# Output projection by chunks onto a residual in PSUM, and other places in the queues

## The reference

```python
x = norm(x + random_feature_attention(x))          # ln1
x = norm(x + cross_attention(x, ctx))              # ln2: 16 heads, 120 keys
x = norm(x + three_cycles_of_coupling(x))          # ln3: gelu nets, out += coupling * twist(out)
# ln4: the state-space part
xr = x @ W_in.T;  x_ssm, res = split(xr)           # 512 channels each
xc = silu(conv4(x_ssm));  delta = softplus(xc)
h[n] = exp(-exp(A_log[n]) * delta) * h[n] + xc*xc  # a scan over the sequence, 16 states
y = xc * sum_n(h[n]) * silu(res) + D * xc
x = norm(x + y @ W_out.T)
x = norm(x + (gelu(x @ ctx.T) * (x @ ctx.T)) @ ctx)  # ln5
x = norm(x + gate * expert[argmax(router(x))](x))  # ln6: 8 experts, all computed
```

## Time and profile before

| what | value |
|---|---|
| median of 3 runs | 3413.72 us (3413.61 to 3415.29) |
| profiled execution, its own time | 3415.3 us |
| span, first to last instruction | 3413.5 us, 41544 instructions |
| busy share of the span: PE, DVE, ACT, POOL | 76%, 74%, 50%, 44% |
| mean granted clock of PE | 0.827 of 2.4 GHz |
| a loop turn | 201.4 us |
| DMA | 45.72 MB, 13 GB/s over the span |

### The profile page before, as it was taken

The page is one execution under the profiler, slowest core; times in us unless marked ns, Lnnn a source line. Parts: engine busy times, 40 slices in busy tenths (PEclk is TensorE's granted clock), DMA queues, the critical chain, the costliest instruction groups (busy, mean ns, idle before and its releaser), DMA issues.

```text
span 3413.5 us, 41544 instructions
## 1 busy us (share of the span) xinstructions
PE 2603.7 (76%) x10956; PEld 1509.9 (44%) x10956; DVE 2515.0 (74%) x4320; ACT 1722.0 (50%) x3078; POOL 1492.6 (44%) x1159
## 2 busy tenths in 40 slices
PE   4985787868778786877878688687877878787556
PEld 2544444444445443444444344444444445444323
DVE  2258678696877869687786968778696886859683
ACT  1456454546546464564646455454655545456430
POOL 1036354463525446253543625355362544526370
PEclk8767798888888888888888889888887988869677
DMA  3000000000000000000000000000000000000000
GB/s 118 10 7 9 13 10 13 15 13 6 9 19 9 13 12 3 19 9 19 9 13 12 3 19 9 13 15 13 12 3 19 9 13 6 7 6 0 12 5 8
DMA packets 16849, 45.72 MB, mean 13 GB/s; under 512 B 2248, under 2 KB 7056, under 8 KB 16400
## 3 DMA queue, kind: packets, MB, share of 16 engines
q1 hardware_dynamic: 16656, 43.96, 3.8%
HBM read 35.57 MB, written 8.39 MB: 13 GB/s over the span
## 4 chain that ended last, share of the span: by engine, by line
PE 47%; DVE 24%; issue 13%; ACT 12%; DVEq 1%; POOL 1%; ACTq 0%; DMA 0%; SPq 0%; POOLq 0%
PE bank L522 45%; DVE h_ring L1065 10%; ACT a_ring L1447 6%; DVE x L1163 2%; DVE smax L969 2%; PE bank L404 1%; ACT spare L1347 1%; DVE qT L1019 1%; DVE couple L1016 1%; DVE x12T L1021 1%; POOL ysum L1635 1%; DVE soft L1044 1%; DVE ln_stats L378 1%; DVE x L396 1%; ACT L1453 1%
## 5 line engine op out<-in xcount | busy, mean ns | idle before, releaser
L1635 POOL TENSOR_TENSOR ysum<-ysum,h_ring 128x512 f32<-128x512 f32 x896 | 1150.3, 1284 | 723.0 <-DVE h_ring L1065 660.3
L1065 DVE TENSOR_TENSOR_SCAN h_ring<-a_ring,bank 128x512 f32<-128x512 f32 x1024 | 1170.0, 1198 | 53.6 <-POOL ysum L1635 43.3
L522 PE MATMUL bank<-w_expert_w,x45T 128*128 128x512 f32 x1024 | 578.3, 712 | 228.1 <-DVE x L1163 226.6
L1447 ACT ACTIVATE a_ring<-soft,decay 128x510 f32<-128x510 f32 x1024 | 651.3, 707 | 25.7 <-DVE h_ring L1065 24.0
L522 PEld LDWEIGHTS bank<-w_expert_w,x45T 128*128 128x128 f32 x1024 | 223.8, 227 | 534.2 <-DVE x L1163 288.4
L1622 POOL TENSOR_TENSOR soft<-xc,soft 128x512 f32<-128x512 f32 x64 | 82.1, 1294 | 748.7 <-ACT soft L1418 748.7
L522 PE MATMUL bank<-x3T,w_winT 128*128 128x512 f32 x512 | 276.3, 673 | 22.5 <-ACT x3T L410 13.1
L522 PE MATMUL bank<-spare,w_cn_w 128*128 128x256 f32 x768 | 235.2, 444 | 74.5 <-ACT spare L1377 64.5
L1163 DVE SCALAR_TENSOR_TENSOR x<-bank,weight,x 128x256 f32<-128x256 f32 x512 | 213.3, 472 | 65.7 <-PE bank L522 65.7
L522 PE MATMUL bank<-qT,kmask 32*120 32x256 f32 x1024 | 215.3, 513 | 57.4 <-ACT spare L1347 56.8
L969 DVE TENSOR_REDUCE smax<-bank 128x4 f32<-128x480 f32 x256 | 156.2, 651 | 118.7 <-PE bank L522 118.7
(11 more groups left out here) (145 smaller groups left out, 4069.2 us busy)
## 6 DMA issues: line engine op xcount, KB each, us to landing
x0T<-in_xT SPq DMA_DIRECT2D x16, 512.0 KB, 3.2
x<-in_x SPq DMA_DIRECT2D x16, 512.0 KB, 3.4
out<-x SPq DMA_DIRECT2D x16, 512.0 KB, 2.8
ctxT<-in_ctxT SPq DMA_DIRECT2D x16, 240.0 KB, 2.5
ctxTb<-in_ctxT SPq DMA_DIRECT2D x16, 240.0 KB, 2.6
ctxb<-in_ctx SPq DMA_DIRECT2D x16, 240.0 KB, 3.0
w_expert_w<-in_expert_w SPq DMA_DIRECT2D x1, 2048.0 KB
w_winT<-in_winT SPq DMA_DIRECT2D x1, 1024.0 KB
```

Source lines behind the costliest of these rows:

```text
L522: return pe.matmul(o, l, r, start=start, stop=stop)
L1065: scanned.then(v.tensor_tensor_scan(h_ring[:, k % HRING, :], a_ring[:, k % RING, :, :].rearrange("p b s -> p (b s)"), xc2, 0.0, ALU.mult, ...
L1447: a.activation(a_ring[:, k % RING, :, 1:S], delta[:, c, :].rearrange("p (b s) -> p b s", b=NB)[:, :, 1:S], ACT.Exp, scale=decay[:, k:k + 1 ...
L1635: p.tensor_tensor(out=total, in0=first, in1=h_ring[:, k % HRING, :], op=ALU.add)\
```

## The change

The output projection goes by channel chunks instead of by tiles. At the end of a turn, after the last coupling cycle and ahead of rotate_back(f, 0), PE puts the residual of m into the banks MB by a product of the identity with the tensor of ln3 (two of 128 x 512), and adds the first three chunks to it. At the head of the next turn it adds the fourth chunk alone. keep and DVE's adds fall away; DVE takes the statistics of ln4 from PSUM and normalises out of PSUM. Beside the waits on the loads two are new: DVE's norm_apply of ln3 waits until PE has read the residual, and PE's transposes of ln4 wait for all four tiles.

Other places in the queues: the last tile of the input projection comes ahead of the last two score tiles; gated_out comes inside the loop of slots (k = 1), and expert_bias behind that loop and the first feature product; ACT's spread of ln4 (norm_rstd) comes ahead of the second input tile's copy; softplus of the last two chunks comes later in ACT's queue, and decays go on between the slots; DVE has other steps of PLAN done between its other work, the last two expert sums and ln6's statistics behind all scans; POOL adds the last two deltas in between its sums; squares are made at the decays 0, 18, 43 and 59. The weights are loaded under three semaphores: five tensors first, then the group's inputs, then those of cross attention and coupling with the head rows, then the rest.

```diff
+DELTA_AFTER = {13: 2, 18: 3}
 OUT_AFTER = 4
-SQUARE_AT = (0, 20, 34, 48)
+SQUARE_AT = (0, 18, 43, 59)
...
+FIRST = ["rfwT", "projT", "rows", "columns", "ident"]
+FRONT = ["wk", "wv", "wq", "wo", "cn_w1", "cn_w2", "cn_w3", "cn_w4", "gc_w1", "gc_w2", "gc_w3"]
+REST = [name for name in WEIGHTS if name not in FIRST + FRONT]
...
+            load_weights(FIRST, loaded_first)
             load_xT(0)
             load_keys(0)
             load_x(0)
+            load_weights(FRONT, loaded_front)
+            sp.dma_start(head_rows[:, :, :], ins["head_rows"]).then_inc(loaded_front.sem, 16)
+            load_weights(REST, loaded_rest)
             load_back(0)
...
-            def mamba_out(g, k0, k1):
...
-                    last = mm(MB[t // 2][:, t % 2 * D:t % 2 * D + D], yT[:, c, t // 2, t % 2 * P:t % 2 * P + P],
-                              woutT[:, c, :], c == 0, c == IC - 1)
-                    if t % 2 and c == IC - 1:
-                        last.then_inc(n4.sub_ready.sem, 1)
+            def mamba_out(g, c0, c1):
+
+                if c0 == 0:
+                    pe.wait_ge(expert_added.sem, expert_added.at(g, 0))
+                    pe.wait_ge(n3.x_ready.sem, n3.x_ready.at(g, NT))
+                    for h in range(2):
+                        mm(MB[h][:, :], ident[:, :], n3.x[:, 2 * h:2 * h + 2, :].rearrange("p t d -> p (t d)"),
+                           True, False).then_inc(resid_ready.sem, 1)
+                for c in range(c0, c1):
+                    pe.wait_ge(scanned.sem, scanned.at(g, AFTER["out", c, 0]))
+                    for t in range(NT):
+                        last = mm(MB[t // 2][:, t % 2 * D:t % 2 * D + D], yT[:, c, t // 2, t % 2 * P:t % 2 * P + P],
+                                  woutT[:, c, :], False, c == IC - 1 and t % 2 == 1)
+                        if t % 2 and c == IC - 1:
+                            last.then_inc(n4.sub_ready.sem, 1)
...
-                    mamba_out(b, 0, 16)
+                    mamba_out(b, IC - 1, IC)
...
+                    pe.wait_ge(n4.x_ready.sem, n4.x_ready.at(b, NT))
                     norm_turn(pe, n4, b, MB)
...
-                    turn_maxima(f)
+                    scores(f, 5, 6)
                 if m is not None:
                     mamba_in(m, b, 7, 8)
-                if b is not None:
-                    gated_out(b)
+                if f is not None:
+                    scores(f, 6, 8)
+                    turn_maxima(f)
                 for k in range(SLOTS + 2):
                     if f is not None:
                         attend(f, k, k + 1)
                     if b is not None:
-                        if k == 7:
+                        if k == 1:
+                            gated_out(b)
+                        elif k == 7:
                             norm_turn(pe, n5, b, MB)
                         elif k == 9:
                             router(b)
                         elif k == 13:
                             turn_weights(b)
-                        elif k == 15:
-                            expert_bias(b)
...
                 if b is not None:
-                    experts(b, 0, 1)
+                    expert_bias(b)
...
                 if b is not None:
-                    experts(b, 1, 2)
+                    experts(b, 0, 2)
...
+                if m is not None:
+                    mamba_out(m, 0, IC - 1)
+                if f is not None:
                     rotate_back(f, 0)
...
             def ln4_sum(g):
-                v.wait_ge(kept_ready.sem, kept_ready.at(g, 1))
-                norm_add(v, n4, g, [(tiles(MB[h]), n4.x[:, 2 * h:2 * h + 2, :]) for h in range(2)])
-                norm_stats(v, n4, g)
+
+                n4.chain.start(v, g)
+                for t in range(NT):
+                    v.wait_ge(n4.sub_ready.sem, n4.sub_ready.at(g, t // 2 + 1))
+                    n4.chain.then(v.bn_stats(n4.stats[:, t, :], MB[t // 2][:, t % 2 * D:t % 2 * D + D]))
...
+            def ln4_apply(g):
+                v.wait_ge(n4.rstd_ready.sem, n4.rstd_ready.at(g, 1))
+                for t in range(NT):
+                    v.tensor_scalar(n4.x[:, t, :], MB[t // 2][:, t % 2 * D:t % 2 * D + D], n4.mv[:, t, 0:1],
+                                    n4.rstd[:, t:t + 1], ALU.subtract, ALU.mult).then_inc(n4.x_ready.sem, 1)
...
+                states(m, 1)
+                if f is not None:
+                    copy_maxima(f)
+                states(m, 3)
                 if b is not None:
                     gated(b)
-                if f is not None:
-                    copy_maxima(f)
-                states(m, 4)
+                states(m, 6)
                 if b is not None:
                     ln5_sum(b)
-                states(m, 6)
+                states(m, 8)
                 if b is not None:
                     norm_apply(v, n5, b)
-                states(m, 9)
+                states(m, 12)
                 if f is not None:
                     normalize_context(f, 0)
-                states(m, 10)
+                states(m, 14)
                 if b is not None:
                     route(b)
-                states(m, 12)
+                states(m, 16)
                 if b is not None:
                     pick_expert(b)
-                states(m, 14)
+                states(m, 22)
+                if f is not None:
+                    normalize_context(f, 1)
                 if b is not None:
                     start_sum(b)
-                states(m, 16)
-                if f is not None:
-                    normalize_context(f, 1)
-                states(m, 18)
+                states(m, 24)
                 if f is not None:
                     ln2_sum(f)
-                states(m, 19)
+                states(m, 25)
                 if f is not None:
                     norm_apply(v, n2, f)
                 if b is not None:
                     combine(b, 0, 2)
...
-                states(m, 26)
+                states(m, 30)
                 if b is not None:
                     combine(b, 2, 4)
...
                     global_base(f)
                     rotate(f, 0)
                     rotate(f, 1)
+                states(m, 34)
                 if b is not None:
                     combine(b, 4, 6)
-                states(m, 33)
+                states(m, 36)
...
-                states(m, 64)
+                states(m, len(PLAN) - 1)
                 if b is not None:
                     combine(b, 14, 16)
                     ln6_stats(b)
-                states(m, len(PLAN) - 1)
...
                 if f is not None:
+                    if m is not None:
+                        v.wait_ge(resid_ready.sem, resid_ready.at(m, 2))
                     norm_apply(v, n3, f)
...
-            def keep(g, b):
-
-                if b is not None:
-                    a.wait_ge(acc_start.sem, acc_start.at(b, 2))
-                a.wait_ge(n3.x_ready.sem, n3.x_ready.at(g, NT))
-                a.copy(n4.x[:, :, :], n3.x[:, :, :]).then_inc(kept_ready.sem, 1)
...
@@ -1480,9 +1513,11 @@
                     norm_copy(a, n1, f, TURN1)
                 if m is not None:
                     norm_copy(a, n3, m, TURN)
-                    mamba_in(m, 0, 2)
+                    mamba_in(m, 0, 1)
                 if b is not None:
                     norm_rstd(a, n4, b)
+                if m is not None:
+                    mamba_in(m, 1, 2)
...
+                    invert_sums(f, 0)
+                decays(m, 16)
                 if m is not None:
                     softplus(m, 2, 3)
-                decays(m, 8)
...
+                decays(m, 18)
                 if m is not None:
                     softplus(m, 3, 4)
...
-                decays(m, 34)
+                decays(m, 36)
...
+                        if k in DELTA_AFTER:
+                            deltas(g, DELTA_AFTER[k], DELTA_AFTER[k] + 1)
```

More of the change, by code:

```diff
@@ L276, in program @@
         x1b, acc = x12, x6
-        loaded_w = sem("loaded_w")
+        loaded_first = sem("loaded_first")
+        loaded_front = sem("loaded_front")
+        loaded_rest = sem("loaded_rest")
         loaded_xT = sem("loaded_xT", 16)
@@ L433, in _, with load_weights @@
         def _(sp):
-            for name in W:
-                sp.dma_start(W[name][:, :], ins[name]).then_inc(loaded_w.sem, 16)
-            sp.dma_start(head_rows[:, :, :], ins["head_rows"]).then_inc(loaded_w.sem, 16)
+            def load_weights(names, signal):
+                for name in names:
+                    sp.dma_start(W[name][:, :], ins[name]).then_inc(signal.sem, 16)
             def at(tensor, g):
@@ L712, in mamba_in @@
                 if j0 == 0:
+                    if g == 0:
+                        pe.wait_ge(loaded_rest.sem, 16 * len(REST))
                     pe.wait_ge(n3.xT_ready.sem, n3.xT_ready.at(g, DC))
@@ L837, in turn @@
                 if f is not None:
-                    scores(f, 5, 8)
-                    turn_maxima(f)
```

(57 more changed lines are left out.)

21 lines of the change are left out of this document (8 added, 13 removed).

## The result

The changed kernel takes 3287.48 us (median of 4 runs, 3271.13 to 3299.46), the kernel before 3414.05 beside it (4 runs, 3413.61 to 3415.29). The ratio is 0.9626, 95% interval 0.9581 to 0.967: faster, and inside the range given for 8 in 10 (3100 to 3345), but above the forecast's own (3150 to 3270), with three fifths of the gain. Its runs lie 0.9% apart, those of before 0.05%. The profiled run took 3281.97, its span 3280.2.

The account below looks back on a forecast made before the run. No engine is full: a turn is a chain of hand-overs, with VectorE idle 44.2 of 201.4 us. Terms of 12 us a loop turn plus start and ends sum to 205.5, giving 3210 us (own range 3150 to 3270; 8 in 10, 3100 to 3345).

Parts of the forecast that it names:

- The start: Kernel start: weights in three loads let VectorE's first weight work begin at 6.9 us, a gain of 16.5.
- Head: Head of the turn: 24 of 32 output matmuls move to the turn's end, so the input projection ends 4.4 us earlier.
- attention: Scores and attention: with the gate early and gated output behind two slots, the second context product comes 2.5 us earlier.
- scans: Five scans and an output step move into VectorE's old waits in the first half: gain 6.6 us a turn, less 0.8.
- new waits: Second half of the turn: later gates and a 3.9 us wait for the square at scan 32, together -2.2 us.
- last rotations: End of the turn: GpSimd ends its adds 1.8 us earlier, so the last rotations get 1.4 us back.
- The fifth norm: In the loop, GpSimd's adds slow it by 3.8 us, held hidden because VectorE soon waits for the softmax sums.
- the end of the turn: Residual products and 24 matmuls take 6.9 us inside TensorE's 10.21 us gap, costing nothing; with the rotations' gain, +1.4.
- rival D: TensorE at half clock through all of attention: 5 us lost a turn, 3455 us, slower; chance 0.04.
- Rival C: GpSimd's adds meet VectorE's rotations 0 to 3 and slow them: gain only 4 us a turn, 3329 us; chance 0.16.
- B: Rival: the clock stays up and attention runs at 2.4 GHz, gaining 19.5 us a turn, 3099 us; chance 0.18.
- E: Rival: the loop doesn't move, as VectorE's waits return elsewhere; only start and ends gain, 3384 us; chance 0.05.

Follow-up runs that it names:

- e4: The changed kernel with four engines' programs written out without loops and GpSimd's add of a row after its second add of states: 3181.9 us, ratio 0.932.
- e5: The changed kernel, loops kept, with only GpSimd's add of a row issued later: 3245.3 us, ratio 0.9529.
- e9_jumps_moved: e5 with the jump back of TensorE, VectorE and ScalarE moved to places where each waits or is ahead: 3214.8 us, ratio 0.9419.

## Why the forecast was right in sign and short in size

**The start** holds: VectorE's first weight work is at 6.31 (forecast 6.9), the gain 17.3 in the trace and 16.4 alone.

```profile
6.31 1.18 DVE L951 TENSOR_TENSOR w_projT<-w_projT,w_rows 128x256 f32<-128x256 f32 x2 [3.90 <-DMA w_ident<-in_ident]
```

**Head, attention, scans, new waits, last rotations** hold as a sum, 11.5 at the last output step of an undisturbed turn against 11.9, though not term by term. With the output projection ended early, 4.4 at the head were to follow; 3.2 came, and 5.4 in e4, so the missing part is the fetch and the add. The last rotations gave 1.2 of their 1.4 (8.79 to 7.56 us from the first operation to the output step). The fifth norm, slowed beside GpSimd, takes 2.57 instead of 1.38, and behind it stands a wait of 0.26, not some 6 to hide it. The queues' moves were worth nearly twice their price, the projection some two thirds of its own: that the sum came so near is luck. With the end of the turn cured (e4) the change is worth 231.6, more than the 204 forecast.

**The step that fell short is the end of the turn**, where the prediction put what comes behind the last output step at "nothing". In the 11 intervals between the spreads of the loop, the gain up to that step sums to 98.3 (forecast 11 x 11.9 = 130.9), and what follows it loses 36.4 (forecast 0). Of the 69 us missing there, at least 36 are this. I asked only whether the 24 matmuls fit into TensorE's gap of 10.21, and they do, at a granted 1.00:

```profile
1104.45 1.98 PE L535 MATMUL bank<-x,w_ident 128*128 128x512 f32 x4 [1.45 <-DVE x L1200]
1106.27 5.34 PE L535 MATMUL bank<-w_woutT,xpad 128*128 128x256 f32 x24
```

I did not ask what else stood beside the removed projection: the three engines' jumps, all issued at this place, and GpSimd's add, which follows the first norm's transposes and now starts 1.0 us behind the third norm's spread instead of 5.6 (1311.43 - 1310.40; 1370.42 - 1364.86 before). With the earlier trace rows at hand part of this could be seen: the 8.84 us of matmuls at the head stood between the jumps and the next hand-over. TensorE's fetch could not: nothing of it is in the loop before.

**The other 33** lie ahead of the output step. 16 are turns 3 and 4, whose attention begins at 1.2 GHz; 13 are the four turns 8, 11, 12 and 13, each behind a gap (as turn 3 is), where the add meets the sixth norm's spread and its 2.2 us fall behind the mark. I gave rival D 0.04 as a state of all turns; a part of it came, in some. The prediction's ground against D, that half-clock stretches in the record end within a turn's slots, did not hold even before: in turn 15 all slots run at 0.50 and take 37.5 us, in the loop 31.5 at 0.73.

```profile
1415.50:1447.00 31.50, 27.29 (x221) 15.34 (x220) 21.02 (x39) 21.44 (x40) 17.71 (x14) 0.73 0.05 16
3023.90:3061.40 37.50, 36.82 (x221) 20.70 (x220) 20.51 (x38) 21.70 (x40) 18.99 (x15) 0.50 0.04 14
```

**Rival C** had the right mechanism at the wrong place. The rotations 0 to 3 are not slowed (0.42 an operation but for one); the norms at the turn's end are. There one VectorE operation of 0.41 us that starts at 1311.37 ends at 1313.95, 0.14 after GpSimd's add of 2.38, and with the add elsewhere (e4, e5) no such operation is left at the turn's end:

```profile
1311.37 2.58 DVE L405 TENSOR_SCALAR x<-spare,ln_mv,ln_rstd 128x256 f32<-128x256 f32 x1
```

By the Trainium skill, "SBUF — State Buffer", section "Who interferes with whom", the loser of the shared port pair (for VectorE in a two-port mode, which `tensor_scalar` can enter) blocks for the whole of the other's operation: that length agrees. By the same sentence whoever issues first has the pair; the record gives starts, not the order of issue, and the operation that it starts 0.06 earlier is the one that stands. That the ports are the cause is argued; that the add's time is, the runs show.

**B and E** are out: attention keeps a stretch at half clock in every turn (the slots of the loop have a granted 0.68 to 0.71), and the loop moved.

## What to carry to other kernels

Before taking work away from a place, list everything that the work covered there: jumps and their fetches, other engines' operations on shared ports, not just the hand-over that waited for it. Put a loop's jump on each engine where that engine waits or is well ahead; the turn is a ring, so it can be cut anywhere. Where two causes sit at one place, removing either shows almost nothing (0.6 and 0.6 in an undisturbed turn here, 3.9 together), so cure both before judging one.

## What the runs showed of the hardware that was not expected

- A jump back can cost its engine a fetch: 2.4 to 2.8 us on ScalarE in every turn, some 7 (4.85 + 2.33) on TensorE in five of twelve, with packets of 16 KB on q8 beside it; without loops, or with the jump elsewhere, no such gap. The Trainium skill, "Runtime: NRT & Kernel Launch", section "Instruction fetch mechanics", has a taken jump stall its engine where the target isn't held any more, and gives TensorE four times the store of the others; the trace agrees, since q14 moves 10 to 14 packets in every turn of the loop and q8 none but in and behind the turns with a gap. Why TensorE's stretch is sometimes kept and sometimes not, no run shows.
- One GpSimd operation of 2.38 us makes a VectorE operation of 0.41 take 2.58.
- Turns of the same program settle at different lengths, 187.6 and 194.2 in e9_jumps_moved, by whether the granted clock rises 10 or 24 us into the same stretch of attention; in the kernel before all loop turns stood at one length, which is why its runs lay so close together (this last is argued, not shown).
